# A decoder layer with routed experts on one Trainium2 core: results of a step are taken at the head of the next one

## The reference

```python
x = layernorm(x + attn(x))        # 16 heads: softmax of q over d, of k over tokens; state = k^T v; out = q state; LN; Wo
x = layernorm(x + xattn(ctx, x))  # 8 heads over 77 context keys, masked softmax, no weights of its own
x = layernorm(x + ffn(x))         # softmax router, 4 of 8 experts per token, 256 -> 1024 -> gelu -> 256
```

## Time and profile before

| | us |
|---|---|
| median of 3 runs | 1247.07 |
| the profiled execution, its time | 1246.88 |
| its span (first to last instruction) | 1245.1 |
| steps 0 to 10, 0 to 88.04 | 88.0 |
| steps 11 to 34, 88.04 to 348.62 | 260.6 |
| steps 35 to 37 up to the first expert product, to 397.30 | 48.7 |
| mixed steps, to 606 | 208.7 |
| expert tiles alone, to 1201 | 595.0 |
| last LayerNorm, to 1245.1 | 44.1 |

### The profile page before, as it was taken

The page is one execution under the profiler, slowest core; times in us unless marked ns, Lnnn a source line. Parts: engine busy times, 40 slices in busy tenths (PEclk is TensorE's granted clock), DMA queues, the critical chain, the costliest instruction groups (busy, mean ns, idle before and its releaser), DMA issues.

```text
span 1245.1 us, 27244 instructions
## 1 busy us (share of the span) xinstructions
PE 1085.3 (87%) x8576; PEld 904.3 (73%) x8576; DVE 730.4 (59%) x1805; ACT 529.6 (43%) x1141; POOL 641.7 (52%) x739
## 2 busy tenths in 40 slices
PE   6668898888875799998899999999999999999960
PEld 3345666665664688887788888888888888888750
DVE  2678968778777576665754444444444444444326
ACT  2767644645562266544333333333333333333214
POOL 3013327656673587747775555555555555544324
PEclk9879989889886899999999999999999999999995
DMA  4453123122122233333544444556544445553335
GB/s 136 156 165 103 45 77 81 42 73 75 49 68 52 51 69 70 70 57 74 67 73 83 78 77 78 78 75 76 81 77 76 77 75 73 80 75 59 61 60 240
DMA packets 159969, 100.63 MB, mean 81 GB/s; under 512 B 106956, under 2 KB 151168, under 8 KB 159840
## 3 DMA queue, kind: packets, MB, share of 16 engines
q1 hardware_dynamic: 129824, 63.21, 20.4%
q0 software_dynamic: 30016, 35.68, 19.4%
HBM read 49.55 MB, written 31.59 MB: 65 GB/s over the span
## 4 chain that ended last, share of the span: by engine, by line
PE 65%; DVE 14%; ACT 6%; issue 5%; POOL 4%; DMA 4%; SPq 1%; ACTq 0%; DVEq 0%; POOLq 0%
PE big L1693 27%; PE big L1712 14%; PE trans L1712 11%; PE big L1730 3%; PE small L1645 2%; POOL rstd L781 1%; PE big L1732 1%; DVE stat L1078 1%; PE trans L1553 1%; POOL slot_records L803 1%; PE small L1658 1%; PE big L1634 1%; ACT pr L941 1%; DVE w_up L1074 1%; DMA w_down<-in_L_ffn_down_w_dram 1%
## 5 line engine op out<-in xcount | busy, mean ns | idle before, releaser
L1693 PE MATMUL big<-xgT,w_up 128*128 128x256 f16 (+1 forms) x3456 | 410.9, 268 | 15.2 <-DMA xgT<-xg 12.3
L925 ACT ACTIVATE h<-big,up_scale 128x512 f32<-128x512 f32 x270 | 185.6, 687 | 452.7 <-PE big L1693 443.6
L1693 PEld LDWEIGHTS big<-xgT,w_up 128*128 x3456 | 326.5, 99 | 59.5 <-issue 19.2
L832 POOL DMA_INDIRECT token_sums<-y,rec x135 | 223.0, 1652 | 262.6 <-ACT y L933 235.2
L1326 DVE TENSOR_SCALAR hh<-h,h_scale 128x512 f16<-128x512 f32 x270 | 133.4, 494 | 331.1 <-ACT h L925 329.2
L1712 PE MATMUL big<-w_down,hh 128*128 x1280 | 219.5, 273 | 2.4 <-DVE hl L1328 2.1
L1328 DVE SCALAR_TENSOR_TENSOR hl<-h,h_scale,hh 128x512 f16<-128x512 f32 x270 | 203.0, 752 | 9.6
L1712 PE MATMUL big<-w_down,hl 128*128 x640 | 175.0, 273 | 0.0
L817 POOL DMA_INDIRECT xg<-token_rows,rec x135 | 137.3, 1017 | 51.6 <-issue 40.5
L1712 PE MATMUL trans<-w_down,hh 128*128 x880 | 150.2, 273 | 2.5 <-DVE hl L1328 2.5
L803 POOL DMA_INDIRECT slot_records<-recs,posi x128 | 133.3, 1042 | 33.9 <-issue 33.6
(11 more groups left out here) (259 smaller groups left out, 1404.3 us busy)
## 6 DMA issues: line engine op xcount, KB each, us to landing
w_down<-in_L_ffn_up_w_dram SPq DMA_DIRECT2D x8, 1024.0 KB, 5.1
w_down<-in_L_ffn_down_w_dram SPq DMA_DIRECT2D x7, 1024.0 KB, 5.6
wqkv_XA<-in_x_dram SPq DMA_DIRECT2D x32, 128.0 KB, 3.1
XRES<-in_x_dram SPq DMA_DIRECT2D x32, 128.0 KB
token_sums<-X SPq DMA_DIRECT2D x32, 128.0 KB
token_rows<-XR SPq DMA_DIRECT2D x32, 128.0 KB
sums<-token_sums SPq DMA_DIRECT2D x8, 512.0 KB, 7.3
out_dram<-sums SPq DMA_DIRECT2D x8, 512.0 KB, 2.6
```

Of the source, the lines that this page charges most:

```text
L832: pool.indirect_dma_start(acc[0:EARLY_BATCHES * N, :] if t < EARLY else acc, bass.IndirectOffsetOnAxis(ap=rec[:, t % RING, j, 0:1], axis=0 ...
L925: act.activation(h[:, i % H_RING, :], psu[up_bank(i)], ACT.Gelu_apprx_tanh, scale=k["up_scale"][:, t:t + 1]).then_inc(gelu_ready, 1)
L1693: ins = pe.matmul(psu[up_bank(i)][:, j * size(t):(j + 1) * size(t)], w[:, ws, c, m:m + P], xgT[:, t % 2, xs * CC + c, 0:size(t)], start=(n ...
```

## The change

- VectorE takes the context values, the router's logits, the state, the positions and `second_sum` of a step at the head of the next step (`left_products`), and the moments of norm 2 there as well. Norms and sums of c0 and c1 are now done one after the other, not interleaved; norm 2 comes behind the heads.
- TensorE turns and routes the second-norm tile one step later (`turn_second(c5)`, `route(c5)`), and a piece's norm product comes behind `project`. ScalarE takes `exp_logits` at the head of the next step, in the mixed steps ahead of `gelu(i)`, and copies the turned probabilities ahead of `split_high`.
- `choose` is parted into `choose` and `count`; choosing, counting, positions and sends have tables of steps of their own (`CHOOSE`, `COUNTED`, `PLACED`, `SENT`). The four tiles of batch 1's second half are now sent at steps 35 and 36, two in each. Pieces 8 to 14 are split in two parts in two steps (`PARTED`).
- `early_slots` moves from step 36 to step 34, `up_factors` and `early_scales` (for two of the three factors) to step 36, the third factor to step 37. Their scratch tiles lie elsewhere, and `rec` has memory of its own.
- SyncE issues `turned_rows` and `records` ahead of `store_tile`, and `load_values` last; GpSimd gathers tile 0 at the head of step 37, ahead of norm 2's inverse deviation, and tile 1 right behind it.
- There are 51 steps instead of 50, so 13 mixed ones; `EARLY` is 20 instead of 19.

The core of the diff:

```diff
-PIECE_STEPS = [2, 3, 4, 5, 6, 7, 8, 9, 11, 13, 15, 19, 23, 28, 32, 35]
-HALF_STEPS = [2 * TB + 2, 2 * TB + 5]
-STEPS = (TB + 1) * (B - 1) + HALF_STEPS[1] + 2
-
-EARLY = 19
+PIECE_STEPS = [2, 3, 4, 5, 6, 7, 8, 9, 10, 12, 14, 18, 20, 23, 30, 35]
+LOAD_STEPS = [1, 2, 4, 5, 6, 7, 8, 9, 10, 11, 13, 17, 19, 23, 29, 34]
+PARTED = range(8, 15)
+CHOOSE, COUNTED, PLACED = (
+    {(0, 0): 19, (0, 1): 23, (1, 0): 28, (1, 1): 32, (2, 0): 37, (2, 1): 40, (3, 0): 45, (3, 1): 49},
+    {(0, 0): 20, (0, 1): 24, (1, 0): 28, (1, 1): 32, (2, 0): 37, (2, 1): 40, (3, 0): 45, (3, 1): 49},
+    {(0, 0): 21, (0, 1): 25, (1, 0): 29, (1, 1): 33, (2, 0): 38, (2, 1): 41, (3, 0): 46, (3, 1): 50})
+SENT = [list(range(23, 31)), [31, 32, 33, 34, 35, 35, 36, 36], list(range(40, 48)), [48, 48, 49, 49]]
+STEPS = PLACED[B - 1, HALVES - 1] + 1
+
+EARLY = 20
 EARLY_BATCHES = 2
 EARLY_TILES = TB * EARLY_BATCHES
-COUNT_STEP = HALF_STEPS[1] + (TB + 1) * (EARLY_BATCHES - 1) + 2
+COUNT_STEP = PLACED[EARLY_BATCHES - 1, HALVES - 1]
...
+                if s >= MIX0 - 1:
+                    turned_rows(s - MIX0 + 1)
+                    if s - MIX0 + 5 < EARLY:
+                        records(s - MIX0 + 5)
                 g = chain_tile(s, 4)
                 if g is not None:
                     store_tile(g)
-                if s == PIECE_STEPS[-1] - 1:
+                if s == LOAD_STEPS[-1]:
                     load_piece(2 * EXP - 1)
                 if s == MIX0 - 2:
                     for t in range(4):
                         records(t)
-                if s >= MIX0 - 1:
-                    turned_rows(s - MIX0 + 1)
-                    if s - MIX0 + 5 < EARLY:
-                        records(s - MIX0 + 5)
+                b, i = divmod(s - TB, TB + 1)
+                if i == 3 and 0 <= b < B:
+                    load_values(b)
...
                 c0, c1, c4 = (chain_tile(s, d) for d in (0, 1, 4))
                 sends = record_sends(s)
+                if s == MIX0 - 1:
+                    gather(0)
                 if c4 is not None:
                     inverse_deviation(2, c4)
+                if s == MIX0 - 1:
+                    gather(1)
                 if s >= MIX0:
                     gather(s - MIX0 + 2)
                 if c0 is not None:
@@ -845,9 +860,6 @@
                     pool.wait_ge(slots_cleared, 16 * (EXP * CAP // (P * INIT_SLOTS)))
                 if c1 is not None:
                     inverse_deviation(1, c1)
-                if s == MIX0 - 1:
-                    gather(0)
-                    gather(1)
                 for b, half, t in sends:
...
+                if c3 is not None:
+                    copy_probs("pa", c3)
+                    copy_probs("pb", c3)
+                if c4 is not None:
+                    high_rows(c4)
+                if c5 is not None:
+                    copy_turned(x2T, "x2", c5)
                 if a is not None:
...
-                if c4 is not None:
-                    high_rows(c4)
-                    copy_turned(x2T, "x2", c4)
-                if c2 is not None:
-                    exp_logits(c2)
                 if square_piece(s) is not None:
...
+                if c3 is not None:
+                    exp_logits(c3)
+                for b, half in at_step(PLACED, s):
+                    shares(b, half)
                 gelu(i)
                 if c1 is not None:
                     copy_turned(zT, "z", c1)
                 if c0 is not None:
                     copy_turned(qT, "q", c0)
-                if c3 is not None and s > MIX0:
-                    exp_logits(c3)
...

+            def left_products(s):
+                c4 = chain_tile(s, 4)
+                if c4 is not None:
+                    value_shares(c4)
+                    value_rows(c4)
+                if s <= MIX0 and chain_tile(s, 6) is not None:
+                    router_logits(chain_tile(s, 6))
+                if s >= 1 and state_built(s - 1) is not None:
+                    build_state(state_built(s - 1))
+                for b, half in at_step(PLACED, s - 1):
+                    take_positions(b, half)
+                if s == COUNT_STEP + 1:
+                    dve.tensor_copy(early_counts[:, :], small_wait(("early",))[:, 0:EXP]).then_inc(sm_free, 1)
+                b, i = divmod(s - TB - 3, TB + 1)
+                if i == 0 and 0 <= b < B:
+                    key_blocks(b)
+                if c4 is not None:
+                    second_sum(c4)
...
+                left_products(s)
                 if close is not None:
                     key_maximum(close)
-                if c4 is not None:
-                    moments(2, c4)
                 if a is not None:
                     take_qkv(a)
+                if c0 is not None:
+                    out_of_heads(c0)
+                    dve.wait_ge(sm_free, SM["out", c0] + 1)
+                    sums_of(0, c0, Z[:, :])
+                    moments(0, c0)
+                if c4 is not None:
+                    norm(2, c4, X2[:, c4 % 3, :], x2_ready)
+                if c1 is not None:
+                    first_sum(c1)
+                    dve.wait_ge(sm_free, SM["wo", c1] + 1)
+                    sums_of(1, c1, X1[:, c1 % 3, :])
+                    moments(1, c1)
...
                 if close is not None:
                     shift_keys(close)
                 if c4 is not None:
-                    norm(2, c4, X2[:, c4 % 3, :], x2_ready)
+                    low_rows(c4)
+                if second_half(s) is not None:
+                    split_low(second_half(s), 1, 1)
                 if c2 is not None:
                     logit_minimum(c2)
-                if c2 is not None:
                     logit_shift(c2)
                 if c1 is not None:
                     norm(1, c1, X1[:, c1 % 3, :], x1_ready)
-                if c3 is not None:
...
+                routing(s)
                 if piece is not None:
-                    split_low(piece)
-                routing(s)
-                if s == COUNT_STEP:
-                    dve.tensor_copy(early_counts[:, :], small_wait(("early",))[:, 0:EXP]).then_inc(sm_free, 1)
+                    split_low(piece, 0, 1 if piece in PARTED else 2)
+                if s == COUNT_STEP + 1:
+                    dve.wait_ge(sm_free, SM[("early",)] + 1)
+                    dve.wait_ge(records_ready, HALVES * EARLY_BATCHES)
+                    early_slots()
                 if s == MIX0 - 2:
-                    dve.wait_ge(sm_free, SM[("early",)] + 1)
-                    early_slots()
+                    up_factors()
+                    early_scales()
                 if s == MIX0 - 1:
-                    factors()
-                    early_scales()
-                if c3 is not None:
...
+                if c5 is not None:
+                    turn_second(c5)
                 if c3 is not None:
                     context_values(c3)
-                if c4 is not None:
-                    turn_second(c4)
-                    route(c4)
+                if c5 is not None:
+                    route(c5)
```

255 lines of the change are left out of this document (119 added, 136 removed).

## The result

The changed kernel takes 1261.06 us (median, 1258.35 to 1261.55), the kernel before 1248.12 on the same chip: ratio 1.010, 95% interval 1.0076 to 1.0123. Forecast were 1221.5 us; the time lies outside the range. The profiled execution has a span of 1256.6 us, 11.5 more than before.

A forecast was written before the change was run, and what follows sets the result against it. TensorE bounds 606 to 1201 us; elsewhere engines wait in turn, so gains come there. From 1245.1: minus 12.6 (steps 11 to 34), 6.8 (steps 35 to 37), 6 (mixed) = 1219.7; plus 1.8 around it, 1221.5 us; range 1203 to 1241.

The forecast's parts named there:

- the terms of the waits (4 us for q, 8 for new ones): Steps 11 to 34: parts of VectorE's 27 us of waits (4 + 3 + 12 + 8), beside 221 us of work.
- the separate order of the two chains: Steps 11 to 34: results of c0 and c1 no longer interleaved add 10 us to VectorE's work.
- the term for q: Steps 11 to 34: VectorE's wait for q from TensorE falls from 20.3 to 4 us.
- The choice of 8: Steps 11 to 34: new waits taken as 8 us, between bounds of 0 and 25.
- the waits only move: Rival, chance 0.20: steps 11 to 34 gain nothing, the switch and mixed steps 12 us together; 1235 us.
- the lock: Rival, chance 0.05: in steps 11 to 34 TensorE stands until VectorE ends splits, routing and head; 1257 us.
- The slower rival: Same rival as the lock, chance 0.05: 1.5 us per step, 36 us over 24 steps; 1257 us.
- about 2 us into step 35: Steps 35 to 37: GpSimd's scatters start then, behind VectorE's head, and the last record leaves at +28.
- the 42 forecast: Step 35 to the first expert product: 42 us instead of 48.7, gain 6.8.
- 15.1 us of new waits: Steps 40 to 47: TensorE waits for ScalarE's copies or up products, with exp_logits ahead of gelu; 15.1 us in all.
- all four holes: Mixed steps: TensorE's tile 1 wait, norm 2 waits, x2 copy waits and two clock falls go; sum 24.4 us.
- the rival that stood on it: Rival, chance 0.04: mixed steps pay a 1.38 us drain at each table change, 22 us in all; 1244 us.

The follow-up runs named there:

- a_slots: a_both with the sixteen slot operations moved from the end of step 34 to the head of step 36; 1241.6 us.
- a_order: a_slots with VectorE taking the two chains of a step interleaved again up to step 37; 1243.8 us.
- b_plus: Kernel before with two needless comparisons added on VectorE at the end of each of steps 11 to 34; 1264.1 us.
- a_early: Changed kernel with VectorE reading a step's small products in the same step again, ahead of routing, up to step 37; 1256.0 us.
- a_both: Changed kernel with the edits of a_early and a_exp together; 1245.4 us.
- b_sp: Kernel before with only SyncE's order changed: turned rows and records ahead of row stores, context values last; 1237.4 us.
- a_exp: Changed kernel with ScalarE taking exp_logits and shares behind the copies of z and q again from step 39 on; 1249.6 us.
- a_nm: a_slots with the norm product of a weight piece ahead of the turn of x1 again, read right behind q, k and v; 1245.0 us.
- a_nopart: a_slots with weight pieces 8 to 14 left whole, in their own step; 1234.1 us.
- a_nmno: a_slots with the edits of a_nm and a_nopart together; 1236.9 us.
- b_parts: Kernel before with only pieces 8 to 14 split in two halves, the second in the next step; 1238.1 us.
- b_fast2: b_sp with slot numbers at the head of step 36, gathers ahead of the powers, records' array kept apart, factors and early scales in step 36; 1230.1 us.

## Why the prediction was wrong

**What bounds the kernel.** Right as far as it went: the stretches in which nobody is full decide, and the pure expert steps hardly moved (TensorE works 587.4 of the 594.3 us from 618.70 on, 588.7 of 595.0 before).

**Steps 11 to 34, the terms of the waits (4 us for q, 8 for new ones).** This is the step that failed first. The sum put 221 us of work and 27 of waits, 8 of them new, with 0 and 25 as bounds. Measured are 213.7 of work and 51.5 of waits. The work was overestimated by 7 us: the separate order of the two chains was counted at 10 us, and a_slots against a_order shows 7.5; and the 4.1 us of slot operations fell behind the stretch, since TensorE opened step 35 at 354.79 and VectorE did them from 359.14 to 363.26. The waits were 24.5 us too low, and that is what failed. The named waits went about as far as forecast for GpSimd (2.0 instead of 3), far less for q (14.9 instead of 4); the new ones are 7.7 us for ScalarE's halves, 3.0 for the positions, 2.9 for the keys. So 10.9 us are missing in the term for q, whose premise was that TensorE goes on to the next projection without VectorE; the rows above show it standing for banks that VectorE had to empty. That these waits and the ones for q are one and the same is argued, not shown. The choice of 8, "nearer to the lower end", had no row, and the reason given (the present waits come from an order that is gone) was an argument for the old waits' going, not against new ones. In a ring of four engines the idle time of VectorE gives way to neither side: it was 53.6 us before, 51.5 after, 53.5 in a_slots, and rose to 64.6 in a_order, where there was less to do; only whole pieces in a_slots (45.2), parts in the kernel before (47.8) and added work (48.7 in b_plus) brought it down. Which wait sets the length of a step was not separated further. The two rivals that had the idle time come back ("the waits only move", 1235 us, and the lock) had 0.25 together; in this stretch they were the case.

**The lock.** The slower rival had the right mechanism and the wrong place. TensorE did stand still until VectorE's head, not ahead of `heads_out` in each of 24 steps (4.5 us in all), but at the third small product of some: positions, turned context, next key maximum, in one to five steps each. The prediction named only the bank ahead of `heads_out` and didn't go through the order of the two banks for the other products, which the change moved too. a_early and a_both show what reading earlier is worth: 5.1 and 4.2 us of the whole, not the 36 of the rival. It took the lock from the switch only; in steps 11 to 34 the same waits stood at other products, and their price stays open.

**Steps 35 to 37.** The chain was right (scatters, landing, records, gather, product), and most links have the sizes that were forecast: 26.2 us for 16 scatters and the powers between them, 2.5 to the records, 2.5 to the gather; the last, 11.4 instead of 8.75, is longer by the bank wait ahead of the turned context (8.4 in a_slots, where that wait is 0.8). Its start is the second step that failed: "about 2 us into step 35" were 15.6. Two things were missing. VectorE is not at the head of step 35 when TensorE opens it: it still had gates and slot operations to do, to 363.26, 8.5 us. The slot operations were entered in steps 11 to 34 at 4.1 us and nowhere else, but they stand ahead of the head of step 35, on which GpSimd's queue waits: a_slots brings the first product 3.7 us forward by moving them. And the scatters stand behind three inverse deviations, the last of which needs the moments of c1, which come behind the head and both chains (to 369.01, 5.7 us more, and 1.4 us to the first scatter); the forecast had the head only. In a_slots the stretch is 49.6 us, 7.6 more than the 42 forecast, and this start alone, 10.4 us instead of 2, is more than that; the other links are 25.8, 2.5, 2.5 and 8.4, together a little less than forecast. What of the 10.4 us could go is not shown. The wait for norm 2 of step 37 behind the gather was forecast at about 4 us and free below 6. It was 4.20 us (6.00 in a_slots) and not free: the route behind it began 2.97 us late, at 406.07, and the turned context stood for its bank until VectorE, which had the choosing and the third factor to do in between, had copied the logits at 411.68.

**Mixed steps.** Right in the waits, wrong in the clock. 15.1 us of new waits were forecast, and the rows for z and h above give 9.3 + 5.8 = 15.1; to the tenth that is luck, since 1.0 us of waits for h were there before. The waits that were to go, 6.45, 4.6 and 7.7 us, are gone. Together this makes TensorE's idle time 4.9 us less than before (68.7 to 63.8). For the clock the sum had 5.7 us of gain (2.3 behind tile 1, 3.4 for two falls) against 3.4 for two new falls. TensorE's busy time is 779.1 us before and 779.8 after: nothing of the gain arrived. The net was -4.2 against -6 forecast. b_sp shows the first hole alone: 10.8 us, 6.6 of them idle time and 4.2 busy time, where the sum had 6.45 and 2.3. a_exp, without the new waits, is 14.2 us shorter than before (847.8 - 833.6), but that is not a test of all four holes: with ScalarE's old order the wait for x2's copy is back (9.8 us).

**The table drain.** The Trainium skill (ScalarE: Activation LUTs, What ACT_TABLE_LOAD costs) adds 1.38 us of drain to each load. The trace of the changed kernel doesn't agree, and the rival that stood on it is out (ScalarE, end of step 42: gelu, load, `exp`):

```profile
497.62 0.69 ACT L938 ACTIVATE h<-big,up_scale 128x512 f32<-128x512 f32 x1 [4.30 <-PE big L1730]
498.32 1.28 ACT L954 ACT_TABLE_LOAD   x1
499.62 1.83 ACT L954 ACTIVATE pr<-big,xmb 128x77 f32<-128x77 f32 x8
```

The load starts where gelu ends, and `exp` 1.30 us later. The order cost 10 us over the eight steps; with the drain of the Trainium skill 22 more would have been due, by the estimate of the prediction.

**The rule of the sum.** The gains were added as if the stretches were separate. a_early and a_exp add (5.1 + 11.5 against 15.7), because they lie in different stretches. In steps 11 to 34 no size of a_order, a_nm and a_nopart followed from the work or the wait that each takes away, though the measured sizes of a_nm and a_nopart add up in a_nmno.

## What to carry to other kernels

Where two engines take turns, moving work gains only if it leaves the ring: go through every buffer that is handed round in order and ask of each product whose release it needs after the move, not only of the one that is first in the step. A table of idle time by releaser says where the slack shows, not what would be saved; measure it by adding known work (b_plus) and by one part alone (b_sp, b_parts), and build the change from the parts that pay by themselves, measuring again after each, since a part can change its sign (the parted pieces). Count the start of a chain from the timeline of the engine that it waits for: VectorE was 8.5 us behind TensorE when TensorE opened step 35. Work needed by a late stage is best put into a wait just before its use (slot numbers and scales in b_fast2, 7 us won on b_sp, with the gathers), not two steps ahead, where it delays everything behind it.

## What the runs showed of the hardware that I had not expected

The time that VectorE needs for the same operations depends on their order by several per cent: the two chains interleaved took 205.5 us in steps 11 to 34, one behind the other 213.0, with the same 622 instructions, and yet the kernel was no faster. Splitting pieces in two parts changed its sign with its surroundings: it won 8.5 us in the kernel before and lost 7.5 in a_slots. And a table load of ScalarE took 1.28 us with nothing measurable beside it (0.01 us from `gelu` to the load).
